# A four-layer model on one core: in the block attention of its first feed-forward stage, the products of exponentials and values are moved directly behind the scores and follow them by two steps where they followed by one

## The reference, cut to what matters

```
light: q, k, v = xn @ wq, xn @ wk, xn @ wv            8 heads of 64, windows of 128 tokens
       out = softmax(q k^T) v, window by window; y = out @ wo
heavy: 256 tokens of each batch are picked by a routing score; their queries
       attend to all 512 tokens of the batch, 8 heads of 64; the result is
       scattered back to the picked rows
```

## Time and profile before

| what | value |
|---|---|
| median of 3 runs | 2548.64 us (2542.93 to 2551.72) |
| span of the profiled execution, first to last instruction | 2534.4 us |
| TensorE matmul busy | 2376.7 us (94%) |
| VectorE busy | 1356.6 us (54%) |
| ScalarE busy | 952.7 us (38%) |
| the chain that ended last, TensorE's part | 82% |
| mean granted TensorE clock | 0.976 of full speed |

### The profile page before, as it was taken

How to read it: one execution, slowest core, us unless ns; L and a number is a source line. 1 busy time by engine, 2 the same in 40 slices (tenths; PEclk the granted TensorE clock), 3 DMA queues, 4 the chain that set the end, 5 groups by cost and what they waited for, 6 DMA issues and landing times.

```text
span 2534.4 us, 38376 instructions
## 1 busy us (share of the span) xinstructions
PE 2376.7 (94%) x13932; PEld 1563.4 (62%) x13932; DVE 1356.6 (54%) x2952; ACT 952.7 (38%) x2231; POOL 594.0 (23%) x548
## 2 busy tenths in 40 slices
PE   6997999999999998998999999978975999999998
PEld 4444676766666665444676655544554777777776
DVE  7886654774445546876456533368873323232322
ACT  2366655444545553332233321234642222222221
POOL 3233222252001002202123100043553111111111
PEclk8998999999999999999999999989987999999999
DMA  5012101021011000100001059202126221222121
GB/s 198 1 35 74 57 9 51 26 89 46 26 43 34 26 26 26 70 1 17 1 1 36 1 169 334 92 0 109 65 84 243 34 35 32 32 34 34 31 34 26
DMA packets 73757, 144.56 MB, mean 57 GB/s; under 512 B 11592, under 2 KB 62536, under 8 KB 71120
## 3 DMA queue, kind: packets, MB, share of 16 engines
q1 hardware_dynamic: 41280, 100.94, 11.6%
q0 software_dynamic: 16368, 26.23, 5.3%
q10 hardware_dynamic: 15936, 15.03, 2.1%
HBM read 107.42 MB, written 71.09 MB: 70 GB/s over the span
## 4 chain that ended last, share of the span: by engine, by line
PE 82%; DVE 10%; ACT 3%; issue 2%; POOL 1%; DMA 1%; SPq 0%; DVEq 0%; POOLq 0%; ACTq 0%
PE PS L2358 13%; PE PS L2380 7%; PE PS L2777 5%; PE PS L1539 4%; PE PS L1530 4%; PE PS L2789 4%; PE PS L2049 3%; PE PS L2061 3%; PE PS L601 3%; PE PS L2846 3%; PE PS L2837 3%; PE PS L2811 3%; PE PS L2882 2%; PE PS L676 2%; DVE mem L1147 2%; DVE mem L1142 2%
## 5 line engine op out<-in xcount | busy, mean ns | idle before, releaser
L2358 PE MATMUL PS<-mem,ctx2T 128*128 x1136 | 350.9, 462 | 4.3 <-SPq L2322 4.3
L2358 PEld LDWEIGHTS PS<-mem,ctx2T 128*128 128x128 f32 x1136 | 211.8, 192 | 111.5 <-issue 7.4
L2540 POOL DMA_INDIRECT out_x<-xnT,moe_small x71 | 110.1, 1551 | 482.6 <-ACT xnT L2435 482.6
L2504 DVE TENSOR_TENSOR ctx2T<-PS,ctx2T 128x352 f32<-128x352 f32 x142 | 74.4, 524 | 247.1 <-PE PS L2358 247.1
L2380 PE MATMUL PS<-mem,moe_small 128*128 x852 | 195.7, 379 | 1.1 <-DVE moe_small L2512 1.1
L2380 PEld LDWEIGHTS PS<-mem,moe_small 128*128 128x128 f32 x852 | 156.4, 190 | 19.9 <-issue 1.4
L1147 DVE RECIPROCAL mem<-PS 128x512 f32<-128x512 f32 x48 | 160.8, 3351 | 13.2 <-PE PS L670 13.1
L2509 DVE COPY moe_small<-PS 128x512 f32<-128x512 f32 x71 | 49.1, 691 | 173.2 <-PE PS L2368 173.2
L1142 DVE TENSOR_REDUCE mem<-PS 128x32 f32<-128x2048 f32 x48 | 109.8, 2288 | 50.3 <-PE PS L626 50.2
L3162 DVE TENSOR_REDUCE moe_small<-PS 128x2 f32<-128x1024 f32 x64 | 78.4, 1225 | 101.8 <-PE PS L2837 101.8
L3307 POOL TENSOR_TENSOR mem<-mem,moe_small 128x512 f32<-128x512 f32 x64 | 82.2, 1304 | 211.5 <-DVE moe_small L3172 211.5
(11 more groups left out here) (378 smaller groups left out, 4574.1 us busy)
## 6 DMA issues: line engine op xcount, KB each, us to landing
slots<-in_trash_rows SPq DMA_DIRECT2D x8, 4290.0 KB, 62.3
mem<-in_L_ffn_experts SPq DMA_DIRECT2D x8, 2176.0 KB, 13.5
xn<-unit_rows SPq DMA_DIRECT2D x15, 512.0 KB, 4.1
xn<-slots ACTq DMA_DIRECT2D x53, 130.0 KB, 2.1
x_all<-in_x SPq DMA_DIRECT2D x8, 512.0 KB, 8.3
mem<-unit_rows SPq DMA_DIRECT2D x8, 512.0 KB, 3.9
out_x<-x_all ACTq DMA_DIRECT2D x8, 512.0 KB, 3.0
unit_rows<-moe_small SPq DMA_DIRECT2D x7, 512.0 KB, 3.2
```

The source lines that it names most:

```text
L2358: last = nc.tensor.matmul(PS[:, 1 + 2 * g + half, 0:HE], m.rowT[:, j % 2, k, :], w[:, :, at:at + HE], start=k == 0, stop=k == KD - 1)
L2540: nc.gpsimd.indirect_dma_start(s.T["out"], bass.IndirectOffsetOnAxis(s.token[:, j % 4:j % 4 + 1], 0), m.result[:, j % 4, :], None, compute ...
```

## The change

No instruction is added, removed or resized. On TensorE, `light_values` and `heavy_values` are called directly behind the scores of a step and two steps after the scores they belong to; before, they were called behind the queries and one step after. On ScalarE, the copy of that product is moved so that it still follows it. Buffers stay as they are: three for the values of tokens, two for the transposed exponentials, one bank for the product.

```diff
@@ colt_pe, light pass
     for j in range(LIGHT_STEPS):
         p, nxt = (light, j + 1) if j + 1 < LIGHT_STEPS else (heavy, 0)
         light_scores(j)
+        if j >= 2:
+            light_values(j - 2)
         keys(p, nxt)
...
         if nxt % CT == CT - 1 and nxt + 1 < LIGHT_STEPS:
             turn_x(light, (nxt + 1) // CT)
-        if j >= 1:
-            light_values(j - 1)
@@ colt_pe, heavy pass
         if u < HEAVY_STEPS:
             heavy_scores(u)
+        if u < 2:
+            light_values(LIGHT_STEPS - 2 + u)
+        elif u <= HEAVY_STEPS + 1:
+            heavy_values(u - 2)
         if u % QT == 0 and nxt < LIGHT_STEPS:
             keys(heavy, nxt)
...
         if u % QT == 1 and nxt < LIGHT_STEPS:
             queries(heavy, nxt)
-        if u == 0:
-            light_values(LIGHT_STEPS - 1)
-        elif u <= HEAVY_STEPS:
-            heavy_values(u - 1)
@@ colt_act, light pass
         light_exponentials(j)
+        if j >= 2:
+            copy_light_oT(j - 2)
...
-        if j >= 1:
-            copy_light_oT(j - 1)
@@ colt_act, heavy pass
         if u % QT == 1 and nxt < LIGHT_STEPS and nxt % CT == 0:
             copy_routed(nxt // CT)
+        if u % QT == 1 and 2 <= u <= HEAVY_STEPS + 1:
+            copy_heavy_oT(u // QT - 1)
         if u % QT == 1 and u <= HEAVY_STEPS:
             copy_probs(heavy, u - 1, 0)
             copy_probs(heavy, u - 1, 1)
         if u < HEAVY_STEPS:
             heavy_exponentials(u)
+        if u < 2:
+            copy_light_oT(LIGHT_STEPS - 2 + u)
...
-        if u == 0:
-            copy_light_oT(LIGHT_STEPS - 1)
-        elif u <= HEAVY_STEPS and u % QT == 0:
-            copy_heavy_oT(u // QT - 1)
```

## The result

The changed kernel is slower by 0.7%: 2564.43 us median (2562.72 to 2566.43, four runs), where the kernel before had 2548.53 us (2542.93 to 2551.72) beside it. The ratio is 1.0072, with a 95% interval from 1.0060 to 1.0084. On a second chip the pair was timed again: 2553.45 us against 2536.19, ratio 1.0073 (1.0059 to 1.0087). So the change costs 16 to 17 us. The two chips differ by 11 to 12 us, whatever the kernel. The first profile of before (span 2534.4 us) fits a chip like the second, so its span and the 2562.6 us of the first profile after, which lie 28 us apart, must not be subtracted. A new profile of before, on a third chip where it takes 2536 us as well, has a span of 2535.1 us.

A forecast was written before the change was run, and what follows sets the result against it. TensorE's queue was taken to bound the kernel, ScalarE's chain setting odd heavy steps. Odd steps +27.1, borders elsewhere +0.7 and light pass -3.0 made +24.8 us on 2548.6: 2573.4 us, range 2557 to 2588.

The forecast's parts named there:

- What bounds: Whole kernel: TensorE's queue sets the time; in odd heavy steps a 3.48 us chain through ScalarE's queue sets the length.
- Scores followed by products: Scores directly ahead of products, at 92 places: taken as 1.06 us, ends 0.95 and 1.15 us, or -10 and +8 us.
- rival of the cheap pair: Scores and products cost no border, 1.72 us a pair instead of 2.08: -33 us, 2540 us; chance 0.04.
- rival of the odd chain that doesn't grow: Odd heavy steps: exponentials gated by the maxima, not the copies, so 1.02 us is absorbed: 2546 us; chance 0.07.
- Plain odd steps: Heavy pass, 8 steps (u = 11, 19, ... 59, and 61): 4.54 to 5.56 us, +1.02 each, +8.2 us.
- u = 5 (mod 8): Heavy pass, 7 steps: second half of `turn_x` waits for `copy_queries`; 5.1 to 6.2 us, +1.1 each, +7.7 us.
- u = 7: Heavy pass, 7 steps at u = 7 (mod 8): 1.02 us plus 0.33 for the product's copy; +1.35 each, +9.5 us.
- u = 1: First odd heavy step: `light_out` waits for the copied last light product; ends near 7.7 instead of 5.9 us, +1.7.
- The borders: Switches of array use: 0.09 us into column halves, 0.20 into row halves; heavy -1.6 and +2.3, light -2.4 us.
- The light pass: Light steps: borders -2.4, DMA wait at j = 18 -1.0, `copy_probs` wait -0.8, steps before j = 5 +1.2; sum -3.0 us.
- The end of the heavy pass: Steps u = 61 to 65: chain of copies equally long in either order, put at 0.
- The clock: Rival: new gaps in the heavy pass lower the granted clock, 2% of 400 us, +8 us: 2581 us; chance 0.10.

The follow-up runs named there:

- act_order: Changed kernel with TensorE's queue kept; in odd heavy steps ScalarE makes exponentials and copies queries before copying the transposed banks: 2528.34 us, ratio 0.9968 to the kernel before.
- light_only: Kernel before with the new order in the light pass alone, the heavy pass keeping the old one: 2526.43 us, ratio 0.9963.
- heavy_only: Kernel before with the new order in the heavy pass alone: 2551.25 us, ratio 1.0062.

## Why the prediction was right, and where it was mis-sized

The direction, the mechanism and the single steps held; the sum was 24.8 us and the change costs 16 to 17. The measured 2564.4 us lie in the range, 9 us under the likeliest 2573. That is in part luck: the lower part of the range stood for a cheaper pair of scores and products, which didn't come, and the error that did come, in the borders, had no term in the range.

- *What bounds.* TensorE's queue in even steps and in the light pass, ScalarE's chain in odd heavy steps. Right, and shown by `act_order`, which moves nothing on TensorE and takes the cost away.
- *Scores followed by products*, taken as 1.06 us, are 1.06 us. The rival of the cheap pair is gone with that. The rival of the odd chain that doesn't grow is gone with the 5.58 us of u = 11.
- *Plain odd steps*: 5.56 us forecast, 5.57 measured. *u = 5 (mod 8)*: 6.2 forecast, 6.11 measured, +1.02 instead of +1.1. *u = 7*: +1.35 forecast, 6.33 us or +1.30 measured. *u = 1*: 7.7 forecast, 7.66 to 7.72 measured. The wait is where it was expected, for the copy of the last light product:

```profile
589.87 0.61 ACT L3005 ACTIVATE mem<-PS 128x512 f32<-128x512 f32 x1
...
590.53 1.99 PE L2882 MATMUL PS<-mem 128*128 128x256 f32 x8 [1.70 <-ACT mem L3005]
```

- *The borders* are the step that was mis-sized. I put 0.09 us on the way into the column halves and 0.20 us on that into the row halves, the latter read from the 1.92 us of `light_out`. In the changed kernel a full group stands ahead of `light_out`, and it takes 1.82 us to the same scores:

```profile
298.96 1.88 PE L2811 MATMUL PS<-xnT,mem 128*128 128x512 f32 x4
300.68 1.89 PE L2882 MATMUL PS<-mem 128*128 128x256 f32 x8
302.50 1.16 PE L2824 MATMUL PS<-mem 64*128 64x128 f32 x16
```

So about 0.10 us is paid on the way in, into either kind of halves, and another 0.10 us by the full group that follows a tiled one. The products between queries and `light_out` cost both. That makes -0.19 to -0.20 instead of -0.09 us in 27 light steps (-5.1, not -2.4) and in 18 heavy steps with an output projection (-3.5, not -1.6), and 0 instead of +0.11 in 21 even steps (0, not +2.3). These three are about 7 us of the 8 us that the sum was too high. The Trainium skill ("TensorEngine Tiling (Array Packing)", Key Properties) says that a change of the tiling mode drains TensorE. The prediction's reading of it, that all such changes cost the same 0.20 us, would have given -5.4 us for the borders of the light pass and was the better guide there. The rows of this case agree with it: a light step has three such changes instead of four and is 0.20 us shorter, and an even step without an output projection has three before and after and stays at 6.66 us.
- *The light pass*: -3.0 us forecast. Its parts in the first profile after are -5.1 (borders), -0.9 (the DMA wait at j = 18 fell from 1.75 to 0.82 us), -0.8 (no wait for L3001) and +1.4 (the steps before j = 5), -5.4 in all. From the first light scores to the first heavy ones it is 328.1 us there, and 333.6 in the new profile of before: -5.5. In the second profile after, the DMA wait is 1.23 us and the pass 328.5 us: -5.1.
- *The end of the heavy pass* was put at 0. It is -1.4 us at u = 62 and +1.1 us behind it.
- *The clock* dipped once in the heavy pass of one of the two profiles after: in the 10 us from 890.00 the granted clock was 0.83, and the even step there took 8.29 us instead of 6.66. In the second profile no such step is found. The rival feared 8 us over the whole pass; the pattern from 790.29 to 842.38 has TensorE busy 92% of the time, as feared, at a granted clock of 1.00. What it is worth is under 2 us in one execution, and no part of the cost of the steps.

```profile
890.00:900.00 10.00, 8.29 (x46) 4.93 (x43) 4.05 (x9) 4.90 (x13) 0.00 (x0) 0.83 0.00 0
```

With the measured parts the heavy pass is 8.2 + 7.1 + 9.1 + 1.8 - 3.5 - 1.4 + 1.1 = +22.4 us; the second profiles of the two kernels show +22.3.

Of the signs named for the profile after, the even steps of 6.66 us and the missing wait for L3001 came as written. The pattern is 52.09 us (52.8 forecast), the wait of the scores for L2977 is 22.7 us in the first profile and 24.2 in the second (25 forecast), and that of `turn_x` about 1.0 us (1.2 forecast).

## What to carry to other kernels

When a group of matmuls is moved, find out what it covered and what it now stands ahead of; here 1 us of products moved ahead of the transposes lengthened 22 of 64 steps by 1.0 to 1.3 us each, and one by 1.8, though TensorE got no more work. An engine that is 38% busy can still set the pace through the order of its own queue: putting the copies that nobody needs yet behind the exponentials took the whole cost back. Groups that use the array in halves were better set side by side: where scores and products became neighbours between full groups, four changes of the array's use became three, and the step lost 0.20 us.

## What the runs showed of the hardware that was not expected

A full-array group behind a tiled one (one that uses the array in halves) is longer than the same group behind a full one: `light_out` took 1.92 us behind the products and 1.82 behind the queries, the transposes 0.93 and 0.87 us. And an attention stage whose code is untouched can take several us more or less: at its start the granted clock was 0.85 in the kernel before and 1.00 in `light_only`, and the totals of `light_only` and `heavy_only` came out about 5 us lower than the changed stage explains. Two executions of the changed kernel differ at the same place by 1.6 us (18.1 and 19.7 us from the last group of products to L620), so a difference of a few us between two profiles isn't by itself the work of a change.
